# A mixture-of-experts tail on one core: token rows kept in SBUF and carrying their routing weight, weighting and NaN handling moved to the expert stage

## The reference, cut to what matters

```python
x = h.reshape(T, D)                       # layer-normed tokens
logits = x @ gate_w + gate_b
probs = softmax(logits); idx = argmax(probs); prb = probs[idx]
one_hot = jax.nn.one_hot(idx, E)
pos = (cumsum(one_hot, axis=0) * one_hot).sum(-1) - 1
kept = pos < C                            # C = 1280
buf = zeros((E, C, D)).at[idx, where(kept, pos, C)].set(x, mode='drop')
hmid = relu(einsum('ecd,edf->ecf', buf, w1) + b1)
ybuf = einsum('ecf,efd->ecd', hmid, w2) + b2
y_tok = ybuf[idx, minimum(pos, C - 1)] * (prb * kept)[:, None]
y = nan_to_num(y_tok, nan=0.0, posinf=10000.0, neginf=-10000.0)
t = t + y                                 # then back to channels first
```

## Time and profile before

| what | us |
|---|---|
| median of 3 runs | 8098.92 |
| lowest and highest | 8095.15, 8099.15 |
| the profiled execution | 8096.61 |
| its span | 8094.9 |
| stage of the MLP (about 6815 to 7215) | 400 |
| scatter (about 7242 to 7331) | 89 |
| expert products (about 7331 to 7925) | 594 |
| gather (about 7930 to 8095) | 165 |

### The profile page before, as it was taken

The page is one execution under the profiler, slowest core; times in us unless marked ns, Lnnn a source line. Parts: engine busy times, 40 slices in busy tenths (PEclk is TensorE's granted clock), DMA queues, the critical chain, the costliest instruction groups (busy, mean ns, idle before and its releaser), DMA issues. The chain is left out here.

```text
span 8094.9 us, 165843 instructions
## 1 busy us (share of the span) xinstructions
PE 6922.9 (86%) x56132; PEld 5006.7 (62%) x56132; DVE 6010.3 (74%) x8278; ACT 4653.5 (57%) x7795; POOL 5808.5 (72%) x4008
## 2 busy tenths in 40 slices
PE   8799999999999994788888888888888876757993
PEld 6677777777777773455555555555555554546882
DVE  4477777777777774899999999999999996640116
ACT  2377767767777762666666666666666663211223
POOL 0188878878888880899999999999999995321006
PEclk9899999999999996889998999889998987978995
DMA  3301011010110005122221112222212222332113
GB/s 106 104 0 27 0 27 27 0 27 0 27 27 0 6 5 190 67 70 72 72 74 67 61 64 73 70 74 67 69 60 70 71 69 73 133 146 77 63 57 129
DMA packets 175718, 489.50 MB, mean 60 GB/s; under 512 B 31894, under 2 KB 70452, under 8 KB 154160
## 3 DMA queue, kind: packets, MB, share of 16 engines
q1 hardware_dynamic: 158256, 442.45, 16.7%
q10 hardware_dynamic: 10880, 25.28, 0.8%
q0 software_dynamic: 6144, 16.33, 0.6%
HBM read 360.72 MB, written 123.73 MB: 60 GB/s over the span
## 5 line engine op out<-in xcount | busy, mean ns | idle before, releaser
L1548 DVE TENSOR_TENSOR_SCAN hh<-mb_ps_da,state,hh 128x512 f32<-128x512 f32 x2016 | 2447.0, 1262 | 78.4 <-POOL hh L1471 55.3
L1471 POOL TENSOR_TENSOR hh<-dtx,bb 128x1024 f32<-128x1024 f32 x1024 | 2401.6, 2370 | 126.4 <-PE mb_ps_y L1175 118.1
L652 POOL TENSOR_TENSOR p_lo<-p_turned 128x512 bf16<-128x512 f32 x2048 | 2086.3, 1040 | 526.9 <-ACT p_turned L618 270.6
L1339 ACT ACTIVATE mb_ps_da<-dt,amat 128x512 f32<-128x512 f32 x2016 | 1372.3, 685 | 1016.1 <-DVE hh L1548 1000.9
L1175 PEld LDWEIGHTS mb_ps_y<-ident,hh 128*128 128x128 f32 x8192 | 1007.0, 150 | 724.9 <-issue 341.0
L545 PE MATMUL ps_s<-k_head,q_tile 64*128 64x512 f32 x4096 | 1383.0, 643 | 57.6 <-POOL q_tile L663 44.3
L1175 PE MATMUL mb_ps_y<-ident,hh 128*128 128x128 f32 x8192 | 1157.1, 289 | 280.1 <-POOL hh L1477 226.3
L671 DVE TENSOR_SCALAR_CACHE_REDUCE prob<-ps_s 128x1024 f32<-128x1024 f32 x1024 | 1248.0, 1219 | 97.0 <-PE ps_s L545 90.5
L611 ACT ACTIVATE prob<-prob,nmx 128x1024 f32<-128x1024 f32 x1024 | 1169.6, 1142 | 27.5 <-DVE nmx L676 27.5
L618 ACT ACTIVATE p_turned<-ps_t 128x512 f32<-128x512 f32 x1280 | 736.4, 596 | 771.8 <-PE ps_t L558 771.8
L558 PEld LDWEIGHTS ps_t<-ident,prob 64*128 64x128 f32 x16384 | 911.0, 139 | 358.4 <-issue 319.3
(11 more groups left out here) (228 smaller groups left out, 8321.2 us busy)
## 6 DMA issues: line engine op xcount, KB each, us to landing
bb<-mb_bc SPq DMA_DIRECT2D x128, 1024.0 KB, 4.7
cc<-mb_bc SPq DMA_DIRECT2D x256, 256.0 KB, 3.2
q_head<-q_full SPq DMA_DIRECT2D x16, 1024.0 KB, 16.2
mb_u<-u SPq DMA_DIRECT2D x32, 512.0 KB, 4.6
m_dirs<-dtx SPq DMA_DIRECT2D x32, 512.0 KB, 8.3
ex_w<-in_L_ffn_w SPq DMA_DIRECT2D x16, 1024.0 KB, 7.6
xbuf<-ml_zero SPq DMA_DIRECT2D x16, 640.0 KB, 5.5
ex_xr<-xbuf SPq DMA_DIRECT2D x40, 256.0 KB, 2.7
```

The lines of the kernel that those rows point to most:

```text
L652: pool.tensor_tensor(lo[:, k, ms, :], pt[:, k, ms, :], hi_view[:, k, ms, 1::2], ALU.subtract).then_inc(lo_ready, 1)
L1339: act.activation(decay(s, q, e), dt[:, j, blk, :], ACT.Exp, scale=amat[:, j, blk, r % S:r % S + 1]).then_inc(da_ready, 1)
L1471: pool.tensor_tensor(hh[:, r % RING], dtx[:, j, half(r // S)], bb[:, r % S, :].unsqueeze(1).broadcast_to([P, HK, CH]), ALU.mult).then_inc( ...
L1548: dve.tensor_tensor_scan(h, a, h, state[:, s.j, q % S, blk:blk + 1], ALU.mult, ALU.add).then_inc(scanned, 1)
```

## The change

`t2` and the normed tokens are kept in SBUF for all 16 chunks (tiles `t2` and `xw`). A row is ROW = 258 values long: 256 of the token, the weight, and a zero; `xbuf` has rows of 1032 bytes. The mlp stage's two stores go to these tiles. The scatter takes its rows from `xw`. The expert chunk copies the two weights of each partition aside (`wc`), adds the bias, multiplies, and makes the NaN handling on 512 values per partition in five operations, before the store to `ybuf`. The last stage clears a buffer for all tokens, gathers with `scat`, so that dropped tokens keep zeros, and adds `t2` by accumulating two transposes in PSUM.

```diff
+ROW = C + 2
 # mlp_phase
-                    sp.dma_start(rows[i + 1], zero[:, :]).then_inc(zeroed, 16)
+                    sp.dma_start(rows[i + 1], zero[:, :].unsqueeze(1).broadcast_to([P, SPAN, ROW])).then_inc(zeroed, 16)
-                    sp.dma_start(xn[i - 1], flat(xcur[:, q])).then_inc(xn_stored[q], 16)
+                    sp.dma_start(of_chunk(xw, i - 1)[:, :, 0:C], xcur[:, q]).then_inc(xn_stored[q], 16)
-                    sp.dma_start(t2[i], flat(t2cur[:, j])).then_inc(t2_stored[j], 16)
+                    sp.dma_start(of_chunk(t2, i), t2cur[:, j]).then_inc(t2_stored[j], 16)
...
 # routing_phase: weight = xw[:, :, C:C + 2]
-            link(dve.reciprocal(weight[:, :], sm[:, :]))
+            link(dve.reciprocal(weight[:, :, 0], sm[:, :]))
+            link(dve.memset(weight[:, :, 1], 0.0))
-            link(dve.tensor_copy(slot[:, :], fslot[:, :]))
...
 # experts_phase, SyncE
-            for n in range(4):
-                load_rows(n)
...
-            for n in range(4, N):
-                sp.wait_ge(scattered[n % 4], 64 * (n // 4))
-                load_rows(n)
-            for j in range(4):
-                sp.wait_ge(scattered[j], 64 * (N // 4))
+            sp.wait_ge(scattered, 64 * N)
...
-                    sp.wait_ge(turned, ONE + n + 1)
+                    sp.wait_ge(x_copied, ONE + n + 2)
...
-                sp.wait_ge(y_added, ONE + (n + 1) * 2)
+                sp.wait_ge(y_safe, ONE + n + 1)
 # GpSimd
-                pool.wait_ge(rows_loaded[n % 4], ONE + 16 * (n // 4 + 1))
-                        in_=rows[:, n % 4, t, :], in_offset=None, bounds_check=EXPERTS * CAP - 1,
-                        oob_is_err=False).then_inc(scattered[n % 4], 16)
+                        in_=xw[:, 4 * n + t, :], in_offset=None, bounds_check=EXPERTS * CAP - 1,
+                        oob_is_err=False).then_inc(scattered, 16)
 # VectorE
+                dve.tensor_copy(wc[:, q, :], xr[:, q, :, C])
                 dve.tensor_copy(xt[:, q], ps_x[:, q, :].rearrange("p (k r) -> p k r", k=2)).then_inc(x_copied, 1)
...
+                dve.wait_ge(y_safe, ONE + n)
+                stand(dve, stood)
                 dve.wait_ge(y_ready, ONE + n + 1)
+                for t in range(2):
+                    dve.tensor_tensor(yr[:, t, :], ps_y[:, t, 0:C], b2c[:, m // M, :], ALU.add).then_inc(y_added, 1)
                 dve.wait_ge(y_stored[q], ONE + r * (TURN // 2) * 16 + m // 2 * 16)
+                dve.wait_ge(y_added, ONE + (n + 1) * 2)
                 for t in range(2):
-                    dve.tensor_tensor(yr[:, q, t, :], ps_y[:, t, 0:C], b2c[:, m // M, :], ALU.add).then_inc(y_added, 1)
+                    last = dve.tensor_scalar(yr[:, t, :], yr[:, t, :], wc[:, q, t:t + 1], None, ALU.mult)
+                last.then_inc(scaled, 1)
+                dve.wait_ge(scaled, ONE + n + 1)
+                y = flat(yr)
+                dve.tensor_tensor(lost[:, :], y, y, ALU.not_equal)
+                dve.tensor_scalar(flat(ys[:, q]), y, 1e4, -1e4, ALU.min, ALU.max)
+                dve.tensor_scalar(fin[:, :], y, 0.0, 0.0, ALU.mult, ALU.is_equal).then_inc(tested, 1)
+                dve.wait_ge(tested, ONE + n + 1)
+                dve.copy_predicated(flat(ys[:, q]), lost[:, :], zero[:, :].broadcast_to([P, 2 * C])).then_inc(limited, 1)
+                dve.wait_ge(limited, ONE + n + 1)
+                dve.copy_predicated(flat(ys[:, q]), fin[:, :], y).then_inc(y_safe, 1)
...
 # gather_phase: y_loaded has one semaphore per chunk; the loads of t2, the weighting, the NaN handling and the add are gone
+            for n in range(N):
+                dve.memset(yg[:, n].rearrange("p t c -> p (t c)"), 0.0).then_inc(zeroed, 1)
...
+            for n in range(N):
+                pool.wait_ge(zeroed, n + 1)
                 for t in range(4):
                     pool.indirect_dma_start(
+                        out=yg[:, n, t, :], out_offset=None, in_=ybuf,
+                        in_offset=bass.IndirectOffsetOnAxis(ap=scat[:, 4 * n + t:4 * n + t + 1], axis=0),
...
-                        last = pe.transpose(ps_o[:, q, k, t * P:(t + 1) * P], tin[:, j, t, k * P:(k + 1) * P], ident[:, :])
+                        pe.matmul(ps_o[:, q, k, t * P:(t + 1) * P], t2[:, 4 * n + t, k * P:(k + 1) * P], ident[:, :],
+                                  start=(t == 0), stop=False, is_transpose=True)
+                pe.wait_ge(y_loaded[n], 64)
+                for k in range(2):
+                    for t in range(4):
+                        last = pe.matmul(ps_o[:, q, k, t * P:(t + 1) * P], yg[:, n, t, k * P:(k + 1) * P], ident[:, :],
+                                         start=False, stop=(t == 3), is_transpose=True)
                 last.then_inc(turned, 1)
```

More of the change, by code:

```diff
@@ L1610, in mlp_phase @@
     N = B * NCH
+    SPAN = EXPERTS * CAP // (N * P)
     FB = 4
@@ L1687, in flat, with of_chunk @@
                 return t.rearrange("p t c -> p (t c)")
+            def of_chunk(t, c):
+                return t[:, 4 * c:4 * c + 4, :] if isinstance(c, int) else t[:, ds(c * 4, 4), :]
             def load_m(c, j):
@@ L1712, in step @@
                     stand(sp, stood)
[L1713 to L1716 removed]
+                    sp.dma_start(of_chunk(t2, i), t2cur[:, j]).then_inc(t2_stored[j], 16)
+            rows = xbuf[0:EXPERTS * CAP, :].rearrange("(n p t) c -> n p t c", n=N, p=P)
             load_m(0, 0)
@@ L1894, in _, with routing_phase @@
             run(dve, step)
-def routing_phase(nc, ctx, lg, tri, slot, scat, weight):
+def routing_phase(nc, ctx, lg, tri, scat, xw):
     def sb(name, shape, dt=F32):
@@ L1910, in routing_phase @@
     pos, kept, fslot, fscat = sb("pos", [P, T]), sb("kept", [P, T]), sb("fslot", [P, T]), sb("fscat", [P, T])
+    weight = xw[:, :, C:C + 2]
     ps_c = ctx.enter_context(nc.psum_tensor("rt_ps_c", [P, T * E], F32))
@@ L2011, in experts_phase @@
     y_stored = [sem(f"y_stored{j}") for j in range(2)]
-    rows = sb("rows", [P, 4, 4, C])
-    rows_loaded = [sem(f"rows_loaded{j}") for j in range(4)]
-    scattered = [sem(f"scattered{j}", 0) for j in range(4)]
+    zeroed, scaled, tested, limited, y_safe = sem("zeroed"), sem("scaled"), sem("tested"), sem("limited"), sem("y_safe")
+    scattered = sem("scattered", 0)
     N = B * NCH
+    flat = lambda t: t[:, :, :].rearrange("p t c -> p (t c)")
     TURN = 2 * M
@@ L2164, in _, with gather_phase @@
                 chunk((E // 2 - 1) * TURN + m, m, E // 2 - 1, last=True)
-def gather_phase(nc, ctx, ident, ybuf, slot, weight, t2, out):
+def gather_phase(nc, ctx, ident, ybuf, scat, t2, out):
     def sb(name, shape, dt=F32):
@@ L2175, in gather_phase @@
     N = B * NCH
[L2176 to L2182, removed]
+    yg = sb("yg", [P, N, 4, C])
     ot = sb("ot", [P, 2, 2, CH])
     ps_o = ctx.enter_context(nc.psum_tensor("ga_ps_o", [P, 2, 2, CH], F32))
-    t_loaded = [sem(f"t_loaded{j}") for j in range(D)]
@@ L2186, in gather_phase, with _ @@
-    y_loaded = [sem(f"y_loaded{j}") for j in range(D)]
-    zeroed, weighed, masked, chosen, kept_step, added, turned, copied = (
-        sem(n) for n in ("zeroed", "weighed", "masked", "chosen", "kept_step", "added", "turned", "copied"))
+    y_loaded = [sem(f"y_loaded{n}") for n in range(N)]
+    zeroed, turned, copied = sem("zeroed"), sem("turned"), sem("copied")
     stored = [sem(f"stored{j}") for j in range(2)]
-    flat = lambda t: t.rearrange("p t c -> p (t c)")
     with nc.Block() as block:
+        @block.vector
+        def _(dve):
+            for n in range(N):
+                dve.memset(yg[:, n].rearrange("p t c -> p (t c)"), 0.0).then_inc(zeroed, 1)
@@ L2246, in _ @@
             for n in range(N):
-                j, q = n % D, n % 2
-                pe.wait_ge(added, n + 1)
+                q = n % 2
                 if n >= 2:
                     pe.wait_ge(copied, n - 1)
-                for t in range(4):
-                    for k in range(2):
-                        last = pe.transpose(ps_o[:, q, k, t * P:(t + 1) * P], tin[:, j, t, k * P:(k + 1) * P], ident[:, :])
+                for k in range(2):
[3 more added lines that the diff above has]
+                pe.wait_ge(y_loaded[n], 64)
+                for k in range(2):
+                    for t in range(4):
+                        last = pe.matmul(ps_o[:, q, k, t * P:(t + 1) * P], yg[:, n, t, k * P:(k + 1) * P], ident[:, :],
+                                         start=False, stop=(t == 3), is_transpose=True)
                 last.then_inc(turned, 1)
@@ L2257, in _ @@
         def _(act):
[L2258 to L2262, removed]
-                    last = act.activation(yg[:, j, t, :], yg[:, j, t, :], ACT.Copy, scale=weight[:, 4 * n + t:4 * n + t + 1])
-                last.then_inc(weighed, 1)
-                if n >= 2:
-                    act.wait_ge(added, n - 1)
-                act.activation(flat(safe[:, q]), zero[:, :], ACT.Copy).then_inc(cleared, 1)
-            act.wait_ge(zeroed, 1)
-            prepare(0)
             for n in range(N):
```

(13 more changed lines are left out.)

42 lines of the change are left out of this document (17 added, 25 removed).

## The result

| kernel | median, us | lowest to highest | executions |
|---|---|---|---|
| before | 8099.03 | 8095.15 to 8100.42 | 4 |
| after | 8014.78 | 8009.4 to 8025.79 | 4 |

The account below looks back on a forecast made before the run. TensorE bounds the products; VectorE and GpSimd, waiting for each other, bound the gather. Terms -69.0 - 7.4 + 18.2 + 4.1 + 8 + 0 = -46.1 gave 8050.5 us profiled, 8053 median, range 8020 to 8088.

Parts of the forecast that it names:

- Gather: Last stage: 64 fetches at 1.30 us without a gap, clears free beside them, then a short tail; -69.0 us.
- Rival (c): Gather: clears, landings or transposes hold fetches at 5.2 + 2 us per chunk; saves only 35, kernel 8087; chance 0.08.
- Scatter: Scatter stage: the row loads go, 3.6 us gained at the start and a stall of 3.85 removed; -7.4 us.
- Rival (d): Scatter: rows of 258 values double GpSimd's issue, 2.03 instead of 0.97; 68 us more, kernel 8121; chance 0.04.
- Expert chunk: Expert products: bias copies behind VectorE's new chain stop TensorE 2.6 us at seven expert starts; +18.2 us.
- the clock: Expert products: TensorE's lower clock after half of the seven pauses, 2.3 us each; +8 us, bounds 0 and 21.
- The last chunk's chain: End of the expert products: VectorE's new operations stand ahead of the last store; +4.1 us.
- Rival (a): Expert starts: bias copies cost little or nothing, so stalls and clock are not paid; kernel 8029; chance 0.15.
- MLP: MLP stage: slower zeros cost nothing within 0.7 us of room before GpSimd's add; 0, bounds +-5 us.
- rival (b): MLP: slower zeros delay a load, GpSimd's add starts behind the fourth activation; 13 x 3.6 = 47 less, 8006; chance 0.10.

Follow-up runs that it names:

- experiment 1: Kernel after, with the zeros written in two pieces of 2580 bytes per partition instead of five of 1032: 8048.95 us, ratio to before 0.9934.
- experiment 3: Kernel before, with the zeros written in five pieces of 1024 bytes per partition: 8093.27 us, ratio 0.9993.
- the kernel before with the wait: Kernel before, with GpSimd's add of the Mamba directions waiting for VectorE's four activations of the chunk before: 8052.69 us, ratio 0.9937.
- experiments 5 and 6: Kernel after: 5 makes GpSimd's Mamba add wait for VectorE's four activations, 8017.39 us; 6 copies the next expert's biases one chunk earlier, 7992.98 us.
- experiment 7: Kernel after, with GpSimd's Mamba add behind VectorE's four activations and the bias copies one chunk earlier: 7982.61 us, ratio to before 0.9852.

## Why the prediction was right and wrong

**Gather: right, -70.0 against -70.9.** Fetches at 1.30 without a gap, clears that cost nothing beside them, and the tail piece by piece. Rival (c) didn't happen.

**Scatter: right, -7.4 against -7.1**, both halves of it: 3.5 at the start and 3.6 for the stall. Rival (d) is refuted by the 0.97 of a scatter.

**Expert chunk: right in mechanism and size.** Pauses of 2.6 were forecast and are 2.33, 16.3 instead of 18.2; the clock was 8, with half of the seven pauses taken by choice, and is 4 x 1.69 = 6.8. That the choice came so near is luck: nothing in the rows told how many would pay. The rest of the 24.9 is 1.8 in small pieces. The last chunk's chain cost 4.1 as forecast: its store is issued 4.93 after the add begins (7905.84 to 7910.77), before it was 0.85. ScalarE's 12.56 named after the bias copy was forecast as 13. Rival (a) is refuted.

**MLP: the step that failed.** "Within that room a slower write of zeros costs nothing. I take 0." The room was taken, and rival (b) came, which had 0.10. Its threshold was placed well: it asked for zeros that take about 1.4 us longer; 1.1 longer, with the load 0.6 later (experiment 1), changes nothing; in the kernel after the zeros take 2.1 longer, the load lands 1.3 later, past the 0.7 of room, and 10 steps of 13 change. Its price of 3.6 for a step is 3.9 by the trace (24.1 to 20.2). It was too large only in that it gave the gain to all 13, and counted no slow product behind a short pause: -37.5 instead of -47. What was wrong was the sentence against it, "a pace that much lower is shown nowhere". That no row showed the pace of pieces of 1032 bytes was no evidence against it; and the prediction had a rule that spoke for it. The Trainium skill (DMA: Bandwidth & Descriptors, "How a descriptor splits into AXI transactions") says that a piece is moved in transactions of 256 bytes, that what is left over takes one of its own, and that a piece which starts off a 256-byte boundary is begun at the boundary below. By that page, and as an estimate, a piece of 1032 bytes takes 5 transactions where one of 1024 takes 4. It was cited and then set to nothing. The traces agree with it in direction: the zeros land after 5.5 in pieces of 1024 bytes (experiment 3), 6.5 in pieces of 2580 (experiment 1) and 7.5 in pieces of 1032 (kernel after). That this splitting is the cause isn't shown; no run has pieces of 1024 bytes that start off such a boundary. With a chance of even a quarter on (b), the range should have reached down to 8006.

## What to carry to other kernels

Where two engines wait for each other, the order in which they meet has a price, and a resource with "room" can pay a *gain* when the room is used up: ask what would be set free if the faster engine waited, and try it with one added wait. When work is added to an engine with idle time, ask what small operation stands behind it on the queue; moving that ahead cost nothing here and gave 22 us. And a transfer whose piece length changes by 8 bytes is a changed transfer, as are all that stand behind it.

## What was not expected of the hardware

The lower clock comes also behind short pauses, and not always. In the kernel after, a pause of 1.41 us was followed by a product of 10.14, and in the kernel before with the wait, one of 1.42 by 10.11, while pauses of 1.30 in the one and 1.46 in the other were followed by products at 2.4 GHz, 7.17 long. Granted clock (the number ahead of the last two) in the stretch of such a product and of a fast one, kernel after:

```profile
7074.20:7081.40 7.20, 7.15 (x34) 6.28 (x35) 4.50 (x10) 0.00 (x0) 2.12 (x1) 1.00 0.16 55
7115.00:7125.20 10.20, 10.13 (x34) 8.34 (x35) 4.51 (x10) 0.00 (x0) 2.13 (x1) 0.70 0.15 51
```

Likewise, seven pauses of 2.33 to 2.41 behind the same work gave a clock of 1.00 three times and about 0.68 four times. What decides is open, and with it the spread between executions: 16 to 24 us in the kernel after and in experiments 5 and 6, but 5 in experiment 7, where the kernel before spreads over 5 in 4 executions and over 13 in 15.
